# A mixture's routing spread over the quads of the attention in front of it, its rows scattered instead of gathered, and its expert loop taken by pairs

## The reference

```
x = x + attention_0(layernorm(x))     # causal, 16 heads of 16 channels, bias on the output
x = x + mixture_0(layernorm(x))       # 64 experts, 6 for each token

# mixture_0
shared = (silu(g) * y) @ w_shared_down            # y, g = halves of x @ w_shared_up, 64 wide
scores = sigmoid(x @ w_gate); topk_idx = the 6 best; w = their scores / their sum
pos    = how many earlier (token, choice) went to the same expert; valid = pos < 128
x_disp[expert, pos] = x[token]                    # 64 experts x 128 rows
out_r  = (silu(g_r) * v_r) @ w_down               # g_r, v_r = halves of x_disp @ w_up, 32 wide
routed = sum over the 6 choices of w * out_r[expert, pos] where valid
result = shared + routed
```

## Time and profile before

| | us |
|---|---|
| median of 3 runs (2999.83 to 3004.7) | 3001.62 |
| the profiled execution, its span | 3010.14, 3008.3 |
| TensorE, VectorE, ScalarE, GpSimd busy | 2607.2, 1955.4, 1547.4, 915.0 |
| mean granted clock of TensorE, as a share of 2.4 GHz | 0.915 |

### The profile page before, as it was taken

How to read it: one execution, slowest core, us unless ns; L and a number is a source line. 1 busy time by engine, 2 the same in 40 slices (tenths; PEclk the granted TensorE clock), 3 DMA queues, 4 the chain that set the end, 5 groups by cost and what they waited for, 6 DMA issues and landing times. The chain is left out here.

```text
span 3008.3 us, 64777 instructions
## 1 busy us (share of the span) xinstructions
PE 2607.2 (87%) x19821; PEld 2195.1 (73%) x19821; DVE 1955.4 (65%) x6103; ACT 1547.4 (51%) x4636; POOL 915.0 (30%) x820
## 2 busy tenths in 40 slices
PE   6984986699996699999967589999999989799996
PEld 5762554566664599999955489999999988467774
DVE  5667323688785688878863567777777788445554
ACT  5885221699995555555562344444554444223332
POOL 2110786201101422222226511111111144536664
PEclk8996755799998799999989799999999999899998
DMA  6003455899401111110114433233323234756777
GB/s 195 2 2 126 90 93 126 291 362 340 170 2 46 63 36 54 36 53 28 36 75 143 177 98 100 86 104 103 102 84 102 82 125 139 320 113 115 116 116 158
DMA packets 241445, 346.39 MB, mean 115 GB/s; under 512 B 30593, under 2 KB 208313, under 8 KB 238113
## 3 DMA queue, kind: packets, MB, share of 16 engines
q1 hardware_dynamic: 202208, 282.08, 29.0%
q0 software_dynamic: 38976, 61.11, 11.0%
HBM read 108.56 MB, written 150.64 MB: 86 GB/s over the span
## 5 line engine op out<-in xcount | busy, mean ns | idle before, releaser
L666 PE MATMUL bank<-norm_t_high,w 128*128 128x256 f32 (+1 forms) x2176 | 446.7, 287 | 8.3 <-DVE w L865 8.3
L830 ACT ACTIVATE probs<-bank,neg_max 128x256 f32<-128x256 f32 (+1 forms) x512 | 224.4, 443 | 407.9 <-DVE inv L946 398.6
L666 PEld LDWEIGHTS bank<-norm_t_high,w 128*128 128x128 f32 x2176 | 363.6, 194 | 9.0 <-issue 9.0
L1269 ACT ACTIVATE probs<-neg_scores,bound 128x256 f32<-128x256 f32 (+1 forms) x768 | 367.0, 486 | 3.8 <-DVE bound L1340 3.2
L666 PE MATMUL bank<-norm_t_low,w 128*128 128x256 f32 (+1 forms) x1088 | 310.2, 285 | 0.0
L1340 DVE CUSTOM_DVE_ANT_0 neg_scores<-bank,table 128x256 f32<-128x256 f32 (+1 forms) x768 | 261.7, 397 | 64.1 <-PE bank L1181 64.1
L981 POOL TENSOR_TENSOR summed<-turned 128x512 f32<-128x512 f32 x64 | 82.5, 1288 | 614.7 <-DVE turned L897 604.9
L726 PE MATMUL bank<-k,q 128*128 128x256 f32 (+1 forms) x1536 | 245.4, 296 | 0.0
L3017 POOL DMA_INDIRECT sums<-norm_ffn x127 | 197.3, 1553 | 156.7 <-ACT norm_ffn L2914 142.1
L952 DVE SCALAR_TENSOR_TENSOR x_sb<-bank,inv,x_sb 128x256 f32<-128x256 f32 (+1 forms) x512 | 224.3, 480 | 29.8 <-DVE inv L946 19.5
L838 ACT ACTIVATE probs_t<-bank 128x384 fp32r<-128x384 f32 (+1 forms) x256 | 139.5, 545 | 199.7 <-PE bank L736 199.5
(11 more groups left out here) (439 smaller groups left out, 6037.7 us busy)
## 6 DMA issues: line engine op xcount, KB each, us to landing
rows<-blank SPq DMA_DIRECT2D x1, 77976.0 KB, 241.1
z<-norm_t_high SPq DMA_DIRECT2D x96, 256.0 KB, 2.5
z<-norm_t_low SPq DMA_DIRECT2D x96, 256.0 KB, 2.5
norm_ffn<-rows SPq DMA_DIRECT2D x127, 152.0 KB, 2.6
weights<-in_experts SPq DMA_DIRECT2D x1, 17024.0 KB, 49.3
q_turned<-halves SPq DMA_DIRECT2D x256, 64.0 KB, 2.0
k_turned<-halves SPq DMA_DIRECT2D x256, 64.0 KB, 2.0
rows<-in_attention SPq DMA_DIRECT2D x7, 1280.0 KB, 6.4
```

The source lines that it names most:

```text
L666: ins = nc.tensor.matmul(out, stationary(a), moving(c), start=(kt == 0 and m == 0), stop=(kt == n - 1 and m == 2))
L830: ins = nc.scalar.activation(probs[j % 2][:, t, 0:width], s_bank[j % 2][:, score_columns(causal, t)], ACT.Exp, bias=neg_max[j % 2][:, t:t ...
L1269: ins = nc.scalar.activation(probs[q % 2][g][:, t, 0:width], neg_scores[g][:, t, 0:width], ACT.Exp, bias=bound[q % 2][:, g, t:t + 1], scal ...
```

## The change

The class `Places` holds the routing of the first mixture and is called from the attention's quads (`dispatch`). Batch b of the first six (`EARLY`) is taken from quad 4b + 7 on: statistics, norm, transposed rows and logits, choice, ranks, gates, one step after the other over six quads, the twelve scatters of a batch in four more quads, three in each, each behind a wait for the attention's progress. The slot of a row in DRAM is expert x 2048 + place; rows have 336 values: 256 channels, 64 gates, zeros and the token's number. Blank rows (64 x 128) are written first by SyncE, ahead of the blanks that were written before too. Transposed rows and logits use free columns of the attention's banks.

In the mixture stage only the last two batches are routed, with 32 scatters; the shared expert stands in front of the loop, with two sets of banks; rows come by plain loads of SyncE. The loop takes experts by pairs, with two up banks. The up product has the weights in the array and the rows moving, so the hidden values come out transposed: each half goes to a strip of 32 partitions, and `transpose_hidden` and `copy_hidden` are gone. `norm_stage`, the sorting and the tables for it are gone from this stage.

```diff
+                    if dispatch:
+                        dispatch.tensor_turn(pe, q - 1, [s_bank[g][:, P:2 * P] for g in range(4)])
...
+                        if dispatch and g == 3:
+                            dispatch.tensor_strip(pe, q, t_bank[1][:, NB:NB + P])
...
+                keys(0)
+                for q in range(QUADS):
+                    b, n = place_of(q)
+                    if n == 0 and b + 1 < B:
+                        keys(b + 1)
+                    dispatch.pool_end(pool, q, ((scores_done, 4 * min(q + 2, QUADS)), (value_done, q), (t_done, 4 * (q + 1))))
...
+    FIRST, PER_BATCH, EARLY = 7, 4, 6
+    STATS, NORMED, TURNED, CHOSEN, RANKED, GATED, SENT = 0, 1, 2, 2, 3, 4, 5
+    SETUP = 7
+    in_front = 4
...
+    def batch_at(self, q, step):
+        b, rest = divmod(q - step - self.FIRST, self.PER_BATCH)
+        last = self.EARLY if step <= self.NORMED else self.EARLY - 1
+        return b if rest == 0 and 0 <= b <= last else None
...
+    def send(self, pool, b, n):
+        t, k = b * QT + n // self.cfg.top, n % self.cfg.top
+        self.nc.gpsimd.indirect_dma_start(self.scratch.rows, bass.IndirectOffsetOnAxis(self.slot[:, t, k:k + 1], 0),
+                                          self.rows[:, t, :], None).then_inc(self.sent, 16)
+    def pool_end(self, pool, q, progress):
+        each = QT * self.cfg.top // self.PER_BATCH
+        for part in range(self.PER_BATCH):
+            b = self.batch_at(q, self.SENT + part)
+            if b is None:
+                continue
+            if b == 0 and part == 0:
+                pool.wait_ge(self.scratch.blank_rows, 16)
+            if part == 0:
+                pool.wait_ge(self.row_ready, b + 1)
+            for n in range(each):
+                pool.wait_ge(*progress[n])
+                self.send(pool, b, part * each + n)
+        b = self.batch_at(q, self.STATS)
+        if b is not None:
+            self.rstd(pool, b)
+        b = self.batch_at(q, self.GATED)
+        if b == self.EARLY - 1:
+            pool.wait_ge(self.row_ready, b + 1)
+            for n in range(self.in_front):
+                self.send(pool, b, n)
...
+    def logits(self, pe, b, target):
+        pe.wait_ge(self.copied, b + 1)
+        for t in range(QT):
+            for kt in range(KT):
+                ins = self.nc.tensor.matmul(target[:, t * self.cfg.E:(t + 1) * self.cfg.E], self.norm_t[:, kt, (b * QT + t) * P:(b * QT + t + 1) * P],
+                                            self.router_w[:, kt, :], start=(kt == 0), stop=(kt == KT - 1), skip_group_check=True)
+        ins.then_inc(self.logits_done, 1)
+    def ranks(self, pe, b, target):
+        row = lambda t: t.rearrange("p t e -> p (t e)")
+        pe.wait_ge(self.chosen_ready, b + 1)
+        self.nc.tensor.matmul(target, self.earlier_bf[:], row(self.chosen_bf[:]), start=True, stop=False, skip_group_check=True)
+        self.nc.tensor.matmul(target, self.ones_bf[:], row(self.seen[:, b * QT:(b + 1) * QT, :]), start=False, stop=True, skip_group_check=True)\
+            .then_inc(self.ranks_done, 1)
...
+    def scalar_begin(self, act, q):
+        b = self.batch_at(q, self.RANKED)
+        if b is not None:
+            self.exponentials(act, b)
+    def scalar_middle(self, act, q):
+        b = self.batch_at(q, self.NORMED)
+        if b is not None:
+            self.normalise(act, b)
...
+    def choose(self, dve, b):
+        nc, E = self.nc, self.cfg.E
+        dve.wait_ge(self.chain, self.count)
+        need(dve, self.ranks_done, b)
+        nc.vector.tensor_tensor(self.chosen_bf[:], self.left[:, :, 0:E], self.padded[:, :, 0:E], ALU.not_equal)
+        self.after(dve, nc.vector.tensor_tensor(self.chosen[:], self.left[:, :, 0:E], self.padded[:, :, 0:E], ALU.not_equal))
+        for t in self.tiles(b):
+            ins = nc.vector.tensor_tensor(self.seen[:, t + 1, :], self.seen[:, t, :], self.chosen[:, t % QT, :], ALU.add)
+            if t == b * QT:
+                self.after(dve, ins)
...
+    def place(self, dve, b):
+        nc = self.nc
+        dve.wait_ge(self.chain, self.count)
+        dve.wait_ge(self.exps_ready, b + 1)
+        nc.vector.tensor_scalar(self.exps[:], self.exps[:], 1.0, None, ALU.add).then_inc(self.chain, 1)
+        self.count += 1
+        self.after(dve, nc.vector.tensor_tensor(self.places[:], self.places[:], self.chosen[:], ALU.mult))
+        for t in range(QT):
+            ins = nc.vector.max(self.slot_best[:, t, :], self.places[:, t, :])
+        self.after(dve, ins)
+        nc.vector.tensor_scalar(self.slot[:, b * QT:(b + 1) * QT, :], self.slot_best[:], -1.0, None, ALU.add).then_inc(self.chain, 1)
+        self.count += 1
+    def weigh(self, dve, b):
+        nc = self.nc
+        dve.wait_ge(self.chain, self.count)
+        self.after(dve, nc.vector.reciprocal(self.exps[:].rearrange("p t e -> p (t e)"), self.exps[:].rearrange("p t e -> p (t e)")))
+        nc.vector.tensor_tensor(self.exps[:], self.chosen[:], self.exps[:], ALU.mult).then_inc(self.chain, 1)
+        self.count += 1
+    def gates(self, dve, b):
+        nc, E = self.nc, self.cfg.E
+        spread = self.inv[:].rearrange("p (t a) -> p t a", a=1).to_broadcast([P, QT, E])
+        dve.wait_ge(self.chain, self.count)
+        self.after(dve, nc.vector.tensor_reduce(self.total[:], self.exps[:], AX.X, ALU.add))
+        self.after(dve, nc.vector.reciprocal(self.inv[:], self.total[:]))
+        nc.vector.tensor_tensor(self.rows[:, b * QT:(b + 1) * QT, C:C + E], self.exps[:], spread, ALU.mult).then_inc(self.row_ready, 1)
...
+    def vector_strip(self, dve, q, source):
+        b = self.batch_at(q, self.CHOSEN)
+        if b is not None:
+            self.read_logits(dve, b, source)
+        b = self.batch_at(q, self.RANKED)
+        if b is not None:
+            self.read_ranks(dve, b, source)
+    def vector_middle(self, dve, q):
+        b = self.batch_at(q, self.RANKED)
+        if b is not None:
+            self.choose(dve, b)
+        b = self.batch_at(q, self.GATED)
+        if b is not None:
+            self.weigh(dve, b)
+        b = self.batch_at(q, self.SENT)
+        if b is not None:
+            self.gates(dve, b)
+    def vector_end(self, dve, q):
+        b = self.batch_at(q, self.CHOSEN)
+        if b is not None:
+            self.pick(dve, b)
+        b = self.batch_at(q, self.RANKED)
+        if b is not None:
+            self.place(dve, b)
+        b = self.batch_at(q, self.STATS)
+        if b is not None:
+            self.statistics(dve, b)
+        b = self.batch_at(q, self.GATED)
+        if b == self.EARLY - 1:
+            self.gates(dve, b)
...
+    def steps_of(enter, up, leave):
+        for n in range(E // 2 + 2):
+            for work, pair in ((enter, n), (up, n - 1), (leave, n - 2)):
+                if work and 0 <= pair < E // 2:
+                    work(2 * pair)
+                    work(2 * pair + 1)
...
+                sp.dma_start(up_w[:], up_in).then_inc(weights_loaded, 16)
+                sp.dma_start(down_w[:], down_in).then_inc(weights_loaded, 16)
+                sp.wait_ge(places.sent, 16 * TILES * TOP)
+                for e in range(E):
+                    if e >= RING:
+                        sp.wait_ge(added[(e - RING) % SUMS], landed(e - RING))
+                    sp.dma_start(tile_rows[e % RING][:], scratch.rows[e * ROOM:e * ROOM + P, :]).then_inc(row_loaded[e % RING], 16)
                 for r in range(SUMS):
...
                 def up(e):
+                    if e == 0:
+                        pe.wait_ge(shared_added, 2 * CHUNKS)
+                        pe.wait_ge(weights_loaded, 32)
                     pe.wait_ge(x_t_copied, e + 1)
-                    need(pe, hidden_ready, e)
+                    need(pe, hidden_ready, e - 1)
                     for kt in range(KT):
-                        ins = nc.tensor.matmul(up_bank[:, 0:2 * H], x_t[e % 2][:, kt, :], up_w[:, e, kt, :], start=(kt == 0), stop=(kt == KT - 1))
+                        for part, rows in enumerate((rows_of(e + 1), rows_of(e))):
+                            ins = nc.tensor.matmul(up_bank[e % 2][rows, 0:P], up_w[:, e, kt, part * H:(part + 1) * H], x_t[e % 2][:, kt, :],
+                                                   start=(kt == 0), stop=(kt == KT - 1))
                     ins.then_inc(up_done, 1)
-                def transpose_hidden(e):
+                def down(e):
                     pe.wait_ge(hidden_ready, e + 1)
-                    need(pe, h_copied, e)
-                    nc.tensor.transpose(h_bank[:, 0:P], hidden[e % 2][:], core.ident[:]).then_inc(h_done, 1)
-
-                def down(e):
-                    pe.wait_ge(h_copied, e + 1)
                     need(pe, product_ready, e - 1)
-                    at = slice(e % PACK * H, e % PACK * H + H)
-                    nc.tensor.matmul(y_bank[e % 2][:, 0:C], hidden_t[e % 2][at, :], down_w[at, e // PACK, :], start=True, stop=True).then_inc(y_done, 1)
-
```

(48 more changed lines are left out.)

474 lines of the change are left out of this document (252 added, 222 removed).

## The result

| | before | after |
|---|---|---|
| median, us (11 runs each) | 3001.36 | 3007.88 |
| the profiled execution, its span, us | 3010.14, 3008.3 | 3007.0, 3005.2 |
| TensorE, VectorE, ScalarE, GpSimd busy, us | 2607.2, 1955.4, 1547.4, 915.0 | 2563.0, 1938.9, 1525.1, 952.1 |

The account below looks back on a forecast made before the run. GpSimd's issuing was taken to pace the loop. Attention +20, way to the first scatter-add -23.4 and loop -52.9 make -56 us: 2954 in the profile, forecast median 2945, range 2920 to 2984 (its own case 2930 to 2960).

Parts of the forecast that it names:

- 2.3 is the sum of the two: Mixture loop: 2.21 us a tile for landing in the same sum plus 0.09 for late landings; 63 intervals are 145 us.
- the third: Rival for the loop: strips do not run side by side, 3.6 us a tile with gaps, 3027 us; chance 0.05.
- The prediction's own sign of being wrong: Loop: scatter-adds waiting for ScalarE at over 2.6 us a tile would show the forecast wrong.
- The 0.09 a tile for late landings: Loop: allowance taken from the last mixture's loop, where late landings cost 10.9 us over 127 scatter-adds.
- forecast 1.7 and 0.25: Loop: TensorE's products at 1.2 GHz, 1.7 us a tile, plus 0.25 for gaps, staying below the loop's pace.
- the further 0.6 us a tile: Loop, strips-in-sequence rival: half a microsecond or more of gaps takes TensorE from 3.0 to 3.6 us a tile.
- The strips: Loop's up products: four 128-column products of a tile go by twos to two strips, 0.85 us instead of 1.7.
- The attention: First attention: routing six batches there adds 3.3 us a batch, 20 us in all; bounds 6 and 36.
- The third quad: Attention: VectorE's routing exceeds its free time, so the third quad grows 1.5 us and the fourth 1.3.
- VectorE's steps: Attention: statistics, small and full-width instructions and a reciprocal of the routing sum to 8 us a batch.
- the second quad: Attention: VectorE has 4.5 us free there, so the quad hides its 2.5 us of routing.
- From stage to first scatter-add: Mixture stage's start to the loop's first scatter-add: 57.7 us against 81.1, bounded by GpSimd's 32 scatters.

Follow-up runs that it names:

- before2: The kernel before, unchanged, run on the first chip for a second profile: 3004.7 us.
- before3: The kernel before, unchanged, run again for a trace from the second chip: its first attention ends at 229.4 us.

## Why the prediction was wrong

The step that failed is "2.3 is the sum of the two". It named two things that can pace the loop when GpSimd doesn't (landing in the same sum, TensorE) and left out the third, the row buffers. That the gathers "become plain loads of SyncE" was costed at nothing in the loop, with no word on what a load waits for: 8 buffers, each free only after a landing, and down products queued behind the transposes of two pairs. The measured term is 193.1 us instead of 145, 48 of the 54 us that are missing. In the kernel before, a gather waited only until the tile eight back had been scaled (`product_ready`): the tokens' numbers for the scatter-add lay in a table of their own (`add_ids`). Now they lie in the row itself, so its buffer is held until the scatter-add has landed, some 4 us after its start. None of the rivals had this either; the third had the sign right and named 3.6 us a tile, 3027 us, for a wrong reason. The prediction's own sign of being wrong did come: scatter-adds that wait for ScalarE (85.1 us by the trace) at over 2.6 us a tile.

Where no ring binds, 2.3 a tile was nearly right: 2.42 with 16 buffers. What was small is the landing in the same sum: mostly 4.6 to 5.3 us from scatter-add to scatter-add, with the row loads beside it, instead of the 4.42 of the earlier trace rows. The 0.09 a tile for late landings, taken from the last mixture's loop, is no measure of it: in it TensorE is busy throughout, so TensorE paces it, and the landings have time to spare. A stretch of that loop in the kernel before, in the columns of the earlier trace rows:

```profile
2750.00:2760.00 10.00, 10.00 (x50) 7.50 (x49) 5.11 (x21) 3.16 (x8) 6.21 (x4) 1.00 0.69 117
```

TensorE was judged rightly, 2.05 us a tile at 1.2 GHz (forecast 1.7 and 0.25), and the further 0.6 us a tile that the prediction weighed for changes of form did not show. The strips do run side by side: the eight up products of a pair take 1.92 us there (396.90), one after the other they would take 3.4, by the forecast's 0.43 for each.

The attention: +21.3 us, forecast 20. Quad by quad, from ScalarE's first copy of one quad to that of the next, before (second profile) and after:

```profile
112.69:119.24 6.55, 5.04 (x60) 3.86 (x58) 4.69 (x25) 5.32 (x21) 3.27 (x3) 1.00 0.00 0
119.24:126.63 7.39, 7.14 (x61) 5.91 (x61) 2.75 (x16) 5.15 (x21) 1.07 (x1) 0.77 0.01 2
126.63:131.90 5.27, 4.95 (x53) 3.77 (x52) 3.91 (x20) 4.50 (x21) 0.00 (x0) 1.00 0.02 5
131.90:137.14 5.24, 4.92 (x59) 3.73 (x56) 3.92 (x20) 5.01 (x19) 0.00 (x0) 1.00 0.01 2
```

```profile
141.99:148.45 6.46, 5.16 (x62) 4.12 (x54) 5.20 (x25) 6.36 (x24) 3.49 (x3) 1.00 0.02 4
148.45:155.99 7.54, 7.30 (x84) 5.79 (x84) 4.79 (x29) 5.21 (x22) 5.84 (x7) 1.00 0.24 91
155.99:162.15 6.16, 4.41 (x38) 3.43 (x38) 5.72 (x30) 4.57 (x21) 4.77 (x5) 1.00 0.41 141
162.15:168.89 6.74, 5.23 (x66) 3.90 (x67) 5.87 (x27) 5.08 (x20) 3.22 (x6) 1.00 0.24 80
```

The third quad grew by 0.9 and the fourth by 1.5 (forecast 1.5 and 1.3), and this batch by 2.4 in all (forecast 3.3). VectorE's steps cost 6.3 us a batch (21.57 less 15.27 in the sums), not 8. But the second quad hides its part only against a batch like this one, where the granted clock before was 0.77. In the batches of before where it did not fall, a batch took 22.9 us, and against those the second quad grew too, by 1.2, and the batch by 4.0. So the total of 21.3 agrees with 20 partly by luck: smaller steps and a second quad that pays made up for each other. The first quad has little free time left, though VectorE is idle in it for 1.3 us: ScalarE is busy 6.36 of 6.46 there, and ahead of the scatters moving VectorE's work into it gained 0.2 us in two quads.

From stage to first scatter-add: 57.8 for 57.7, with GpSimd's 32 scatters as the bound; the last of them ends 44.5 us after the stage's start, as forecast (3, 40.5 and 1). The landing and first load took 4.0 instead of 5.1 us and the way to the first scatter-add 9.4 instead of 8.1, which cancel out. Not foreseen was the gap of 4 us in front of the stage, where before had 0.9; without the scatters of the attention it is 1.5.

## What to carry to other kernels

When a step of a loop changes its source (a gather becomes a load), write down for each buffer of its ring who frees it and what stands in front of that in every queue on the way. Count how many tiles go round in one turn: the pace is the turn by that number, whatever the engines' busy shares say. Taking tiles by pairs doubles how far the queue is ahead, and so left four of eight tiles to a turn instead of six; 10 buffers instead of 8, or the down products ahead of the transposes in the queue, took the loop from 199 to 154 us.

## What the runs showed that was not expected

The same scatters in the same places cost the attention 22 us on one chip, and no cost is seen on another: a batch takes 31 to 34 us with them in all six profiles of the second chip, 26.9 without them there, and 26.9 with them in the profile after and in the three of the first chip, or 1.6 more where the granted clock fell. The first attention of the kernel before, which has no scatters, ends at the same time on both. Its last attention has 96: from the first scatter to the last it took 215.4 us on the first chip (before2) and 246.0 on the second (before3).

```profile
L2519 POOL DMA_INDIRECT rows<-rows,slot x96: 956/960/1070, 2410.8 to 2626.2; - x96
```

```profile
L2519 POOL DMA_INDIRECT rows<-rows,slot x96: 954/960/1070, 2421.5 to 2667.5; - x96
```

That is 31 of the 41 us by which this kernel's profile is longer on the second chip. In the changed attention there, VectorE's copy of the logits stood for 6.54 us (16 row and 8 product buffers), and without scatters for 2.69:

```profile
158.21 0.29 DVE L1654 COPY padded<-bank 128x128 f32<-128x128 f32 x1 [6.54 <-remote]
```

```profile
154.46 0.29 DVE L1653 COPY padded<-bank 128x128 f32<-128x128 f32 x1 [2.69 <-PE bank L1203]
```

TensorE had made the logits at 153.9. VectorE ran on only at 158.2, behind a row of scatters at 152.45, 153.71, 154.98 and 156.24, and GpSimd itself went on at 158.40. What holds VectorE there the trace doesn't name, and it wasn't settled. The later end of the attention, 24 us in the two profiles of the change, is most of the difference between 1.0023 of before in the first comparison and 1.0139 on the second chip; the loop was 6 us longer there too. The version with 16 row buffers beats the kernel before on the first chip (2970.6 against 3006.2 us); on the second, the ones with more row buffers or the turned order only reach it, and the one with the weighing moved beats it by 14 us.
